# Four layers of cross attention on one core: the next batch's inputs loaded in the last MLP, another order of projections in layers 0 to 2, and the fourth maximum of a group behind PV

## The reference

```python
x = L0(x, ctx)        # LN; 16 heads of 32, key mask; o + residual; LN, MLP (gelu, 2048 wide), residual
x = L1(x, ctx, mask)  # 32 heads of 16 on 8 key heads, dense mask added; o + residual; LN
x = L2(x, ctx)        # keys and values of LN(ctx); 16 heads of 32; x + tanh(gate) * o
x = L3(ctx, x)        # keys and values of the 1024 tokens [ctx, x], queries of x, key mask;
                      # o + residual; RMS norm, MLP, + residual
# each attention: softmax(scale * q @ k.T (+ mask)) @ v per head
```

## Time and profile before

| what | us |
| --- | --- |
| runs | 4213.79, 4190.5, 4199.37 |
| median of the runs | 4199.37 |
| the profiled execution | 4186.91 |
| its span in the trace | 4185.3 |
| PE busy | 3692.9 (88% of the span) |
| PEld / DVE / ACT / POOL busy | 1776.0 / 1524.4 / 1180.7 / 293.1 |
| mean granted clock of PE | 0.964 |

### The profile page before, as it was taken

The page is one execution under the profiler, slowest core; times in us unless marked ns, Lnnn a source line. Parts: engine busy times, 40 slices in busy tenths (PEclk is TensorE's granted clock), DMA queues, the critical chain, the costliest instruction groups (busy, mean ns, idle before and its releaser), DMA issues. The chain is left out here.

```text
span 4185.3 us, 39566 instructions
## 1 busy us (share of the span) xinstructions
PE 3692.9 (88%) x14128; PEld 1776.0 (42%) x14128; DVE 1524.4 (36%) x2792; ACT 1180.7 (28%) x1404; POOL 293.1 (7%) x228
## 2 busy tenths in 40 slices
PE   5898988889799898898979989889897998989989
PEld 2445543434344454343434445434343444533434
DVE  2415533540341553354034055335403405443530
ACT  1312323331131232333113123233412312423330
POOL 3000010100000001010010000100001000011000
PEclk9999999999899999999989999999998999999999
DMA  6322143511632214351163221535116222153501
GB/s 125 72 86 42 26 76 59 87 29 50 122 68 91 42 21 78 59 85 29 50 127 67 85 42 21 91 52 78 29 53 132 65 83 39 21 107 49 84 11 61
DMA packets 151761, 271.10 MB, mean 65 GB/s; under 512 B 15520, under 2 KB 22372, under 8 KB 151544
## 3 DMA queue, kind: packets, MB, share of 16 engines
q1 hardware_dynamic: 151556, 268.35, 31.6%
HBM read 152.95 MB, written 4.19 MB: 38 GB/s over the span
## 5 line engine op out<-in xcount | busy, mean ns | idle before, releaser
L922 ACT ACTIVATE pt<-score_banks 128x1024 f32<-128x1024 f32 x768 | 758.2, 1022 | 917.0 <-PE score_banks L783 480.2
L653 PE MATMUL bank<-xT,w 128*128 128x512 f32 x1664 | 750.4, 597 | 30.9 <-ACT xT L895 23.2
L1052 DVE TENSOR_REDUCE mcol<-bank 128x1 f32<-128x512 f32 x528 | 357.8, 688 | 361.1 <-PE bank L751 357.1
L653 PEld LDWEIGHTS bank<-xT,w 128*128 128x128 f32 x1664 | 313.2, 191 | 381.6 <-issue 361.1
L779 PE MATMUL score_banks<-qs,ks 99*128 99x512 f32 (+1 forms) x1280 | 434.3, 416 | 40.1 <-DMA qs<-nm_lo 22.7
L852 PE MATMUL score_banks<-w,wide 128*128 128x512 f32 x1024 | 443.4, 592 | 0.0
L1035 DVE TENSOR_REDUCE mcol<-score_banks 128x2 f32<-128x1024 f32 x248 | 302.0, 1223 | 321.6 <-PE score_banks L742 304.7
L751 PE MATMUL bank<-ks,qs 97*128 97x512 f32 (+1 forms) x784 | 337.0, 443 | 53.7 <-DVE mcol L1052 31.1
L1049 DVE CUSTOM_DVE_ANT_0 bank<-bank,wide 128x512 f32<-128x512 f32 x416 | 284.5, 707 | 257.7 <-PE bank L751 257.1
L779 PEld LDWEIGHTS score_banks<-qs,ks 99*128 99x128 f32 (+1 forms) x1280 | 236.1, 192 | 185.5 <-ACT pt L922 72.4
L1112 DVE TENSOR_TENSOR score_banks<-score_banks,r_down 128x512 f32<-128x512 f32 x32 | 22.4, 699 | 795.6 <-PE score_banks L852 795.6
(11 more groups left out here) (110 smaller groups left out, 2994.0 us busy)
## 6 DMA issues: line engine op xcount, KB each, us to landing
ks<-k_high SPq DMA_DIRECT2D x136, 256.0 KB, 5.7
w<-in_up SPq DMA_DIRECT2D x32, 1024.0 KB, 5.1
w<-in_down SPq DMA_DIRECT2D x32, 1024.0 KB, 5.3
qs<-q_high SPq DMA_DIRECT2D x112, 256.0 KB, 6.7
ks<-k_full SPq DMA_DIRECT2D x72, 256.0 KB, 7.1
w<-in_v SPq DMA_DIRECT2D x16, 1024.0 KB, 5.3
w<-in_q SPq DMA_DIRECT2D x16, 1024.0 KB, 7.9
qs<-q_full SPq DMA_DIRECT2D x64, 256.0 KB, 6.5
```

Source lines behind the costliest of these rows:

```text
L653: last = nc.tensor.matmul(o[:, :], wt[:, c, cols[0]:cols[1]], src[:, c, :], start=(c == 0), stop=(c == NC - 1))
L922: nc.scalar.activation(pt[:, i % PTB], score_banks[:, 2 * (i % 2):2 * (i % 2) + 2, :], ACT.Exp, scale=L.scale).then_inc(exp_done, 1)
L1052: ins = nc.vector.tensor_reduce(col, bank[:, :], AX.X, ALU.max)
```

## The change

- Loads of the next batch: the context tokens, `x` (now into `xn`, the upper half of the tile `v`) and the first two weights (`AHEAD`) are loaded in the MLP of layer 3, behind the steps `down(0)` and `down(1)` and behind the last uses of the weights whose slots they take. Batch 0 has them loaded ahead of the loop; the host pads `x` and `ctx` by a copied batch, so that the last batch loads something too. The end of a batch waits for these loads (`next_in`) and no longer for the stores; that wait stands at the head of the next batch on SyncE, and frees `x` for VectorE (`x_free`). Norm and residual of layer 0 read `xn`.
- Weights: v, k, q in place of v, q, k for layer 0.
- Layer 0: k(0) goes ahead of the norm's transposes, between v(0) and v(1); k(1) goes ahead of q(1).
- Layer 1: two of the four transposes of the mask go behind q(0).
- Layer 2: 16 early pairs of maxima in place of 14; k(0), v(0), v(1), then the transposes of x, q(0), and k(1), v(2), q(1), v(3) and the rest behind it.
- PV stages: of each group's `part`, the first three pieces stand ahead of PV as before, any from the fourth on (`part[3:]`) behind PV and heads.

```diff
@@ -44,2 +44,3 @@
 RING = 2
+AHEAD = 2
 
@@ -72,3 +73,3 @@
 
-WEIGHTS = [(0, "v"), (0, "q"), (0, "k"), (0, "o"), (1, "k"), (1, "v")] + mlp_weights(0)
+WEIGHTS = [(0, "v"), (0, "k"), (0, "q"), (0, "o"), (1, "k"), (1, "v")] + mlp_weights(0)
 WEIGHTS += [(1, "q"), (3, "vc"), (1, "o"), (2, "k"), (2, "v"), (2, "q"), (2, "o")]
@@ -125,13 +126,13 @@
         done = 16
-        steps = [("ctxT", c) for c in range(NC)] + [("norm", 0, "x"), v(0), v(1)] + [("xT", 0, "z", c) for c in range(NC)]
-        steps += in_parts([q(0), k(0), q(1), k(1), v(2), v(3), q(2), k(2), q(3), k(3)], early(done), 18)
+        steps = [("ctxT", c) for c in range(NC)] + [("norm", 0, "x"), v(0), k(0), v(1)] + [("xT", 0, "z", c) for c in range(NC)]
+        steps += in_parts([q(0), k(1), q(1), v(2), v(3), q(2), k(2), q(3), k(3)], early(done), 17)
     elif n == 1:
         done = 12
-        steps = [("maskT", c) for c in range(NC)] + [("xT", 1, "x", c) for c in range(NC)]
-        steps += in_parts([q(0), q(1)] + [v(t, 3) for t in range(NT)], early(done), 10)
+        steps = [("maskT", 0), ("maskT", 1)] + [("xT", 1, "x", c) for c in range(NC)] + [q(0), ("maskT", 2), ("maskT", 3)]
+        steps += in_parts([q(1)] + [v(t, 3) for t in range(NT)], early(done), 8)
     elif n == 2:
-        done = 14
-        steps = [("aT", c) for c in range(NC)] + [("norm", 1, "out"), k(0), v(0), v(1), k(1), v(2), v(3)]
+        done = 16
+        steps = [("aT", c) for c in range(NC)] + [("norm", 1, "out"), k(0), v(0), v(1)]
         steps += [("xT", 2, "x", c) for c in range(NC)]
-        steps += in_parts([q(0), q(1), k(2), q(2), k(3), q(3)], early(done), 9)
+        steps += in_parts([q(0), k(1), v(2), q(1), v(3), k(2), q(2), k(3), q(3)], early(done), 16)
     else:
@@ -160,3 +161,3 @@
         ahead = [("score", n, *divmod(2 * (g + 1) + i, L.slots)) for i in range(2)] if g + 1 < len(groups) else []
-        steps += part[0:1] + ahead[0:1] + part[1:2] + ahead[1:2] + part[2:]
+        steps += part[0:1] + ahead[0:1] + part[1:2] + ahead[1:2] + part[2:3]
         steps += ([("pv_half", n, u, kt)] if n != 1 else []) + [("pv", n, u, kt)]
@@ -164,2 +165,3 @@
             steps.append(("heads", n, u))
+        steps += part[3:]
     steps += [("o", n, t) for t in range(NT)]
@@ -240,2 +242,3 @@
         cx = v[:, 0:NT, :]
+        xn = v[:, NT:2 * NT, :]
         wide = sb("wide", [P, 2, NC, D])
@@ -298,3 +301,6 @@
 
-        x_in, ctx_in, mask_in, out_stored = sem("x_in"), sem("ctx_in"), sem("mask_in"), sem("out_stored")
+        first_in = ctx.enter_context(nc.semaphore("first_in"))
+        out_stored = ctx.enter_context(nc.semaphore("out_stored"))
+        next_in, x_free = sem("next_in"), sem("x_free")
+        ctx_in, mask_in = sem("ctx_in"), sem("mask_in")
         keymask_in = sem("keymask_in")
@@ -466,2 +472,17 @@
 
+        def weight_source(i):
+            n, name = WEIGHTS[i]
+            if name[:2] == "up":
+                f = int(name[2:])
+                src = A[f"up{n}"][:, f * D:(f + 1) * D]
+            elif name[:4] == "down":
+                f = int(name[4:])
+                src = A[f"down{n}"][f * D:(f + 1) * D, :]
+            else:
+                src = A[f"{name[0]}{n}"]
+            return src.rearrange("(c p) n -> p c n", p=P)
+
+        def weight_slot(i):
+            return w[:, i % WSLOTS, :, 0:weight_source(i).shape[2]]
+
         with nc.Block() as block:
@@ -469,4 +490,10 @@
             def _(sp):
+                sp.dma_start(cx, A["ctx_2048"][0].rearrange("(t p) d -> p t d", p=P)).then_inc(first_in, 16)
+                sp.dma_start(xn, A["x"][0].rearrange("(t p) d -> p t d", p=P)).then_inc(first_in, 16)
+                for i in range(AHEAD):
+                    sp.dma_start(weight_slot(i), weight_source(i)).then_inc(first_in, 16)
                 for dst, src in CONSTS:
                     sp.dma_start(dst, src, allow_slow_non_contiguous=True).then_inc(const_in, 16)
+                sp.sem_inc(out_stored, 16 * NT)
+                sp.wait_ge(first_in, 16 * (2 + AHEAD))
 
@@ -510,22 +537,10 @@
                 def _(sp):
-                    def tokens(ap):
-                        return ap[bass.ds(b, 1)].rearrange("o (t p) d -> p (o t) d", p=P)
+                    def tokens(ap, at=b):
+                        return ap[bass.ds(at, 1)].rearrange("o (t p) d -> p (o t) d", p=P)
 
                     def load_weights(i):
-                        n, name = WEIGHTS[i]
                         if i >= WSLOTS:
                             wait_weights_used(sp, *WEIGHTS[i - WSLOTS])
-                        if name[:2] == "up":
-                            f = int(name[2:])
-                            src = A[f"up{n}"][:, f * D:(f + 1) * D]
-                        elif name[:4] == "down":
-                            f = int(name[4:])
-                            src = A[f"down{n}"][f * D:(f + 1) * D, :]
-                        else:
-                            src = A[f"{name[0]}{n}"]
-                        sp.dma_start(w[:, i % WSLOTS, :, 0:src.shape[1]], src.rearrange("(c p) n -> p c n", p=P)
-                                       ).then_inc(w_in[i % WSLOTS], 16)
+                        sp.dma_start(weight_slot(i), weight_source(i)).then_inc(w_in[i % WSLOTS], 16)
 
-                    sp.dma_start(cx, tokens(A["ctx_2048"])).then_inc(ctx_in, 16)
-                    sp.dma_start(x[:, :, :], tokens(A["x"])).then_inc(x_in, 16)
                     sp.dma_start(m8[:, :], A["mask8"][bass.ds(b, 1), :]).then_inc(keymask_in, 16)
@@ -534,4 +549,7 @@
                                  ).then_inc(keymask_in, 16)
-                    for i in range(WSLOTS):
+                    for i in range(AHEAD, WSLOTS):
                         load_weights(i)
+                    sp.wait_ge(out_stored, 16 * NT)
+                    nc.sync.sem_clear(out_stored)
+                    sp.sem_inc(x_free, 1)
                     sp.wait_ge(keymask_set, 1)
@@ -596,4 +614,15 @@
                                 sp.dma_start(row["beta1"], bcast(A["L1_xattn_beta"], D)).then_inc(gamma_in, 16)
-                        if step in LAST_USE and LAST_USE[step] + WSLOTS < len(WEIGHTS):
-                            load_weights(LAST_USE[step] + WSLOTS)
+                        elif kind == "down" and n == 3 and step[2] < 2:
+                            sp.wait_ge(norm_done, N_NORM[("norm", 3, "mid")])
+                            if step[2] == 0:
+                                sp.dma_start(cx, tokens(A["ctx_2048"], b + 1)).then_inc(next_in, 16)
+                            else:
+                                sp.dma_start(xn, tokens(A["x"], b + 1)).then_inc(next_in, 16)
+                        if step in LAST_USE:
+                            i = LAST_USE[step] + WSLOTS
+                            if i < len(WEIGHTS):
+                                load_weights(i)
+                            elif i - len(WEIGHTS) < AHEAD:
+                                wait_weights_used(sp, *WEIGHTS[i - WSLOTS])
+                                sp.dma_start(weight_slot(i - len(WEIGHTS)), weight_source(i - len(WEIGHTS))).then_inc(next_in, 16)
                     for t in range(NT):
@@ -602,3 +631,3 @@
                                      ).then_inc(out_stored, 16)
-                    sp.wait_ge(out_stored, 16 * NT)
+                    sp.wait_ge(next_in, 16 * (2 + AHEAD))
 
@@ -633,3 +662,3 @@
                 def _(pe):
-                    landed = [0]
+                    landed = [AHEAD]
 
@@ -639,3 +668,3 @@
                             k = landed[0]
-                            pe.wait_ge(w_in[k % WSLOTS], 16 * (k // WSLOTS + 1))
+                            pe.wait_ge(w_in[k % WSLOTS], 16 * (k // WSLOTS + (k % WSLOTS >= AHEAD)))
                             landed[0] += 1
@@ -667,3 +696,2 @@
                             if kind == "ctxT":
-                                pe.wait_ge(ctx_in, 16)
                                 src, c = cx, step[1]
@@ -970,8 +998,6 @@
                         if what == "ctx":
-                            dve.wait_ge(ctx_in, 32)
-                        if what == "x":
-                            dve.wait_ge(x_in, 16)
+                            dve.wait_ge(ctx_in, 16)
                         if what == "out":
                             dve.wait_ge(gamma_in, 32)
-                        src = cx if what == "ctx" else (v if (n, what) == (3, "mid") else x)
+                        src = cx if what == "ctx" else (v if (n, what) == (3, "mid") else xn if what == "x" else x)
                         dst = {"out": x, "ctx": cx}.get(what, zrow)
@@ -1103,3 +1129,5 @@
                                 own(nc.vector.tensor_tensor(bank[:, :], bank[:, :], row[f"o{n}"][:, :], ALU.add))
-                                ins = nc.vector.tensor_tensor(dst, bank[:, :], x[:, t, :], ALU.add)
+                                if (n, t) == (0, 0):
+                                    dve.wait_ge(x_free, 1)
```

(9 more changed lines are left out.)

## The result

The changed kernel takes 4174.16 us (median of 8 runs, 4159.14 to 4178.44), the kernel before 4196.08 (8 runs, 4186.95 to 4213.79): a ratio of 0.9939, interval 0.9918 to 0.9959. The forecast was 4130 and -69 us; the time went down by 22, a third of that, and lies just inside the upper end of the stated range (4085 to 4175).

What follows compares the result with a forecast made beforehand. TensorE was taken as the bound, with gains only where it idles, waits or runs at low clock. Terms of -19.3 us in three batches, -18 in the first and +7 for loads gave -69: 4130, range 4085 to 4175.

Steps and rivals of the forecast that it cites:

- Loads and start: Batch boundary and layer 0's start: TensorE starts 7.5 us earlier, the transposes of the normed x 6.0 earlier.
- Rival 3: At the batch start, the mask and norm chain is the bound, 2.5 us late per batch: -59, 4140; chance 0.05.
- Rival 4: At the batch boundary, semaphore clearing and jump shorten too, 7.1 us a batch more: -97, 4102; chance 0.03.
- the 7.1: Batch boundary: us left after store issuing for clearing semaphores, barrier and jump back, which the change was to leave whole.
- Heads of layers 0 and 2: From projections to first score: new orders save 6.0 us a batch in layer 0 and 9.3 in layer 2.
- Layer 1's PV stage: Moved maxima queue behind heads on VectorE and transposed maxima wait longer: +8.5 us a batch.
- rival 2: Low clock spreads behind up to six new waits a batch, about 5 us each: +51, 4250; chance 0.08.
- The sign that I had set: Layer 1's PV stage: granted clock still above 0.9 if the forecast holds.
- Layer 3: PV stage: one moved transpose right before its score stalls 4.7 us instead of 2.5; in all +1.8 a batch.
- pass no stacking DMA in PV: SyncE's queue: column-transpose DMAs move with their steps and overtake no stacking DMA in PV; costed at nothing.
- Layer 1's head: Moving q(0) ahead of two mask transposes saves 1 us a batch, bounds -4 and +2.
- the 7 allowed for slower stacks: Heads: weight loads slow the stacking DMAs, +1.75 us a batch, bounds 0 and 6; +7 in the sum.

Runs made afterwards that it cites:

- e_move_off: The changed kernel with the move behind PV undone in all layers, loads and head orders kept: 4100.84 us, ratio 0.9753 to the kernel before.
- e_move_02: The changed kernel with the move behind PV kept in layers 0 and 2, undone in layers 1 and 3: 4092.09 us, ratio 0.9740 to the kernel before.
- e_move_only: The kernel before with the move behind PV alone, in all layers, without loads ahead or new head orders: 4260.11 us, ratio 1.0154.
- e_move_012: The changed kernel with the move behind PV undone in layer 3 alone: 4138.62 us, ratio 0.9858 to the kernel before.
- e_l1_heads: `e_move_02` plus layer 1's move only in the six groups that end a unit (eight maxima behind heads): ratio 0.9786 to the kernel before.
- e_l1_noheads: `e_move_02` plus layer 1's move only in groups that do not end a unit (25 maxima, two column transposes): ratio 0.9735 to the kernel before.
- e_l1_before_heads: `e_move_02` plus layer 1's move, its pieces placed behind PV but ahead of heads: 4088.61 us, ratio 0.9738 to the kernel before.
- e_move_023: The changed kernel with the move behind PV undone in layer 1 alone: 4123.79 us, ratio 0.9817 to the kernel before.
- e_l3_k: `e_move_02` plus layer 3's move of the two k projections alone: ratio 0.9743 to the kernel before.
- e_l3_maxT: `e_move_02` plus layer 3's move of one instruction, the transposition of unit 3's column of maxima: ratio 0.9746 to the kernel before.
- e_best_l1head: `e_move_02` with layer 1's head in the old order: 4079.02 us, ratio 0.9715 to the kernel before.

## Why the prediction was wrong

**Loads and start: right.** Idle at the boundary 9.32 (forecast near 9), 4.50 to the first projection (4.55), 12.41 for the three projections (12.85), the norm done 12.4 after TensorE's start (12.5). The first q came some 5 earlier a batch (6.0). Rival 3 falls: the cover over the norm was 4.5, not 1.4. The 1.4 was a slip: by the prediction's own 4.55 and 12.85 TensorE gets there 17.4 after the barrier, not 13.9, which leaves 4.9. Rival 4 falls too: the boundary gained 7.4, and of the 7.1 put down to clearing, barrier and jump 6.8 are still there, from 1052.24 to 1059.03. That the jump's cost stayed agrees with the rule on branches of the Trainium skill ("Runtime: NRT & Kernel Launch", section "Instruction fetch mechanics"); no run here split the 7.1.

**Heads of layers 0 and 2: right in the main.** Layer 0's head -3.9 on the mean (forecast -6.0), its PV stage -3.7 (-1.9); of layer 2, head -7.3 with the transposes of a before it (-9.3) and PV stage -6.5 (-5.4). With the move undone layer 0's PV stage is as short (`e_move_off`, 62.4), with 1.0 more idle and 1.1 less busy time than in `e_move_02`; on the kernel before, the move alone shortens it by 3.0 (`e_move_only`, 63.5). So it did shed waits there, but the -1.9 is not what makes this stage short, and that its sign came out beside the head's share is in part luck. What layer 0's head lacks is clock: at a granted clock of 1.00 it took 45.8 to 46.2 in seven batches of the runs, the forecast being 46.8; in this kernel it ran at 0.90 to 0.96.

**Layer 1's PV stage: right in the waits, short in the price.** The forecast for it was +8.5, all of it waits, with waits behind heads of 0.9, 1.3, 2.4, 0, 0.9 and 2.8. Measured behind the same units: 0.77, 1.21, 2.16, 0, 0.77 and 2.60. TensorE's waits in that stage in the changed kernel:

```profile
PE bank L779 <- DVE mcol L1075: 9.1, 8, 2.6
PE bank L790 <- issue: 4.5, 5, 0.9
PE bank L790 <- DVE mcol L1075: 2.4, 2, 1.3
...
PE bank L779 <- DMA ks<-q_full: 2.0, 1, 2.0
...
PE bank L682 <- DVE mcol L1075: 1.2, 1, 1.2
```

The transposed columns wait 6.9 (forecast 7.9, before 4.1) and the maxima 10.3 with q(2). But the stage grew by 12.9, 6.4 of it idle and 6.5 at the low clock. I knew that price from the earlier trace rows, 10.2 us at 0.50 after a wait of 2.73, and put it into rival 2 alone, by the number of such waits, and not into the sum of this stage. The sign that I had set, a clock of this stage above 0.9, was too coarse: it stayed at 0.92 to 0.96.

Windows of 6 us show which waits the low clock followed. The 2.16 ends in the first row here (at 1469.12), the 1.21 just before the second (at 1436.20):

```profile
1468.00:1474.00 6.00, 4.88 (x15) 3.75 (x15) 3.11 (x9) 1.02 (x1) 0.00 (x0) 0.73 0.00 0
...
1438.00:1444.00 6.00, 5.29 (x23) 2.50 (x22) 1.78 (x5) 2.34 (x3) 1.28 (x1) 1.00 0.01 2
```

In the changed kernel, `e_move_012` and `e_l1_heads` such windows show a lowered clock behind the 2.60 in all twelve batches (0.50 to 0.75) and around the 2.16 in eleven, and behind the 0.77, the 1.21 and the other 0.77 in none; where nothing waits behind heads (`e_l1_noheads`, `e_l1_before_heads`) there is none at these places. So two of the five waits brought it. A term that is counted in a rival should stand in the sum with its share: at rival 2's 5 a wait these two make 10 a batch, against 6.5 measured and none in the sum.

**Layer 3: the step that failed.** I costed one moved transposition, at +1.8 (its terms add up to 2.25, and the 0.45 taken off as "small" has no row). Moved were besides eight maxima and two k projections, for which I saw only the cover that they give heads (-0.95), and not SyncE's weight load behind them. So unit 2's score waited longer too, 3.01 instead of 1.22, and unit 3's 3.13 (forecast 4.7 for the transpose and it, against 4.20 measured: 1.07 and 3.13). The first row is of the kernel before, unit 2:

```profile
1901.92 0.74 PE L779 MATMUL score_banks<-qs,ks 99*128 99x512 f32 x2 [1.22 <-DMA qs<-nm_lo]
...
1887.28 1.22 PE L807 MATMUL score_banks<-qs,ks 99*128 99x512 f32 x2 [3.01 <-DMA qs<-nm_lo]
...
1931.91 2.07 PE L807 MATMUL score_banks<-qs,ks 99*128 99x512 f32 x4 [3.13 <-DMA qs<-nm_lo]
```

After the last the clock was 0.50 for 6 us (the last of the first table of windows). The stage cost +7.1. In this stage of the changed kernel, of `e_move_023`, `e_l3_k` and `e_l3_maxT` all 24 waits of 3.0 to 3.1 have a lowered clock behind them (0.50 to 0.82 in the lowest window of 6 us), and so have some of the 1.1 to 1.5 at the same scores; the sum allowed 1 for it. The statement that column-transpose DMAs "pass no stacking DMA in PV" looked at their order alone, not at how close they come to the load in front of them.

**Layer 1's head: wrong in sign.** Forecast -1, bounds -4 and +2; the windows gave +1.1 on the mean, and `e_best_l1head` against `e_move_02` 2.9 a batch with the PV stage behind it. The mean head was 48.3 to 50.0 in the eleven kernels profiled by stages with the new order and 47.8 to 48.1 in the four with the old. Which wait makes the difference was not tried.

**The sum.** Against the forecast, by stages a batch: layer 1's PV stage 4.4 over, its head 2.1, layer 3's PV stage 5.3, layers 0 and 2 together 2.1, and 2.8 in layer 3's head, the last MLP and layer 1's projections, where the clock varied. That is 16.7, 67 in four batches, from which the 7 allowed for slower stacks behind the weight loads go off: 60 (no run measured that allowance by itself), about the difference between -69 and the -9.9 of the profiled pair. Between medians it was 47, since before's profiled run lay low and after's high among theirs.

**What stays open.** Layer 1's move costs 10.5 in `e_move_012`, but its two halves 7.8 and -1.2. The idle time adds up (6.1 and 0.8 against 6.5), the busy time doesn't (1.7 and -2.0 against 3.9). The low clock that three of four batches of `e_move_02` show some 120 us into the stage is gone with the second half alone, and back in two batches with both; why was not tried. Nor was it tried why the start of layer 2 took 12.8 in most batches with layer 1's move and 10.38 without.

## What to carry to other kernels

When steps are moved in an order that all engines share, list for each the instructions that queue behind it on every engine: here heads on VectorE stood before the moved maxima, and a weight load on SyncE before a small DMA that TensorE waits for. Price a new wait of TensorE of 2 to 3 us with the low clock that may follow, in the sum and not in a rival alone: here it followed nearly all the new waits of that length in layers 1 and 3, and none of the shorter ones behind layer 1's heads. And where a change has parts, some good parts can hide a bad one: the loads and heads alone were worth 104 us, and with the move kept in layers 0 and 2 they are worth no less (109 by the ratio, alike within the noise).

## What the runs showed of the hardware that I had not expected

The length of one stage fell into separate groups, without any difference in its order: the head of layer 0 took 45.8 to 46.2, 47.7 to 47.9, 48.4 to 49.1 or 50.3 to 50.6 in the 52 batches of the runs profiled by stages with the new order, with a granted clock of 1.00, 0.96, 0.93 and 0.90. A small row of 8 KB, issued 2.4 or 4.0 behind a load of 1 MB, landed 0.3 to 0.4 after that load both times, 6.9 and 5.3 after its own issue.
